# Gate and up products of a feed-forward layer by Strassen's seven products, with three-pass float32 matmuls

## The reference

```
h = _layernorm(x, axis=-1) * (1 + cb) + sb
x = x + gb * _L0_ffn_ref(h, L0_ffn_w_gate, L0_ffn_w_up, L0_ffn_w_down)
...
gate = jnp.einsum('bsd,hd->bsh', x, w_gate)
up = jnp.einsum('bsd,hd->bsh', x, w_up)
gated = jax.nn.silu(gate) * up
return jnp.einsum('bsh,dh->bsd', gated, w_down)
```

## Time and profile before

| | |
|---|---|
| median of 3 runs | 1060.18 us (1058.08 to 1065.53) |
| the profiled execution | 1063.38 us |
| its span | 1061.6 us |
| PE busy | 1022.6 us, 96% |
| DVE, ACT, POOL busy | 626.2, 375.0, 225.8 us |
| granted TensorE clock | 0.995 of full speed |
| projections, recurrence, feed-forward | 0 to about 340, to about 505, from 517 us |

### The profile page before, as it was taken

The page is one execution under the profiler, slowest core; times in us unless marked ns, Lnnn a source line. Parts: engine busy times, 40 slices in busy tenths (PEclk is TensorE's granted clock), DMA queues, the critical chain, the costliest instruction groups (busy, mean ns, idle before and its releaser), DMA issues.

```text
span 1061.6 us, 20179 instructions
## 1 busy us (share of the span) xinstructions
PE 1022.6 (96%) x8112; PEld 822.1 (77%) x8112; DVE 626.2 (59%) x997; ACT 375.0 (35%) x685; POOL 225.8 (21%) x178
## 2 busy tenths in 40 slices
PE   6999999999998999998899999999999999999998
PEld 4676777777676888887777887888888888888886
DVE  5977377899855787878664333343333334334366
ACT  3676674445445343333453112211212212112110
POOL 1322530022025555554301000000000000004191
PEclk9999999999999999999999999999999999999999
DMA  6604336838256666775520001010100101001223
GB/s 212 196 14 135 73 80 165 247 100 215 64 125 170 141 153 146 188 187 130 174 72 28 1 1 60 1 60 1 33 28 1 60 1 58 2 0 70 80 80 119
DMA packets 153438, 97.42 MB, mean 92 GB/s; under 512 B 93569, under 2 KB 130689, under 8 KB 153217
## 3 DMA queue, kind: packets, MB, share of 16 engines
q1 hardware_dynamic: 153344, 96.12, 32.9%
HBM read 64.64 MB, written 31.46 MB: 91 GB/s over the span
## 4 chain that ended last, share of the span: by engine, by line
PE 73%; DVE 10%; DMA 5%; issue 4%; ACT 4%; SPq 4%; POOL 0%; DVEq 0%; ACTq 0%
PE ps L1302 70%; ACT t L1665 3%; PE ps L1310 3%; DVE t L1936 2%; DVE t L2046 2%; DMA scrU<-t 2%; SPq L1179 1%; DVE t L2034 1%; PE ps L1539 1%; DVE t L1941 1%; DVE t L2146 1%; DVE t L1946 1%; DMA scrA<-t 1%; SPq L1239 1%; DMA t<-scrA 1%
## 5 line engine op out<-in xcount | busy, mean ns | idle before, releaser
L1302 PE MATMUL ps<-t,t 128*128 128x512 f32 (+6 forms) x7292 | 969.7, 325 | 30.4 <-DVE t L1936 8.5
L1302 PEld LDWEIGHTS ps<-t,t 128*128 128x128 f32 (+4 forms) x7292 | 769.6, 159 | 215.1 <-issue 43.8
L1936 DVE TENSOR_TENSOR t<-ps,t 128x512 f32<-128x512 f32 (+2 forms) x288 | 199.6, 710 | 245.8 <-PE ps L1302 219.5
L1665 ACT ACTIVATE t<-t 128x512 fp32r<-128x512 f32 (+10 forms) x339 | 189.1, 579 | 308.8 <-DVE t L1936 206.2
L1936 DVE TENSOR_TENSOR t<-t,t 128x512 fp32r<-128x512 f32 (+14 forms) x210 | 168.1, 805 | 114.0 <-ACT t L1665 106.6
L1665 ACT ACTIVATE t<-ps 128x512 f32<-128x512 f32 (+5 forms) x202 | 109.1, 551 | 303.0 <-PE ps L1302 285.1
L2427 POOL TENSOR_TENSOR t<-t,t 128x512 f32<-128x512 f32 x16 | 22.5, 1408 | 375.2 <-DVE t L1936 373.1
L2046 DVE SCALAR_TENSOR_TENSOR t<-ps,t,t 128x511 f32<-128x511 f32 (+2 forms) x108 | 80.2, 747 | 3.3 <-ACT t L1665 0.5
L1665 ACT ACTIVATE t<-ps,t 128x512 f32<-128x512 f32 (+2 forms) x93 | 54.5, 617 | 26.1 <-PE ps L1310 13.0
L1310 PE MATMUL ps<-t,t 128*128 128x128 f32 (+1 forms) x340 | 52.3, 285 | 4.2 <-DVE t L1941 2.1
L1310 PEld LDWEIGHTS ps<-t,t 128*128 128x128 f32 (+1 forms) x340 | 38.1, 146 | 13.5 <-issue 5.5
(11 more groups left out here) (52 smaller groups left out, 257.2 us busy)
## 6 DMA issues: line engine op xcount, KB each, us to landing
scrU<-t SPq DMA_DIRECT2D x60, 256.0 KB, 2.9
t<-in_wf SPq DMA_DIRECT2D x16, 768.0 KB, 4.4
t<-scrU SPq DMA_DIRECT2D x32, 288.0 KB, 5.0
t<-scrU SPq DMA_DIRECT2D x32, 192.0 KB, 3.6
t<-in_W SPq DMA_DIRECT2D x19, 256.0 KB, 3.0
t<-in_x SPq DMA_DIRECT2D x16, 256.0 KB, 4.0
t<-in_wmod SPq DMA_DIRECT2D x4, 1024.0 KB, 6.3
t<-in_x SPq DMA_DIRECT2D x32, 128.0 KB, 2.9
```

The costliest lines, as they stand in the source:

```text
L1302: return e.matmul(o, l, r_, start=start, stop=stop, skip_group_check=True)
L1665: return e.activation(o, i, f, **kw)
L1936: return e.tensor_tensor(o, a, b, op)
```

## The change

Gate and up are computed by Strassen's scheme in Winograd's form. A block of 256 hidden units x 512 inputs is cut into 2 x 2 pieces of 128 x 256, two sequences of 512 tokens (1024 columns) into 2 x 2 pieces of 256 x 512. Seven products of such pieces (6 matmuls each) take the place of eight. The products are added in PSUM: `GU` gives for each the product's number and its bank (0 to 2 for gate, 3 to 5 for up). Products 1, 6, 7 and 4 are added one on another in the first bank, and between them ACT copies the bank's state out (`copy_s`); DVE adds these copies to the other two banks (`cadd`). That gives four output tiles: three come out of `cadd`, the fourth is the first bank itself.

The weights' sums and differences are made on POOL (`w_comb`, 4 instructions of 256 columns for gate and 4 for up), the high parts on ACT (`w_high`, 1792 columns), the low parts on POOL (`w_low_ff`, 7 pieces of 256 columns; `w_high_d` for down, 4 pieces). The activations' sums are made on POOL (`t_raw`) and DVE (`t4`), their seven splits by `split_h` (1024 columns each). The feed-forward layer runs in two passes over the weights (16 iterations `it`: 0 to 7 for sequences 0 and 1, 8 to 15 for 2 and 3). Units of sequences 0 and 1 are turned inside the recurrence (`turn_unit`, called with u - 3 at u = 3, 4, 7, 8, 11, 12 and with 12 and 13 at u = 15) and scaled on ACT; the tiles of sequences 2 and 3 are turned in iterations 1 and 2. The ring of the down product has two banks (6 and 7). The first half of the output is stored at iteration 8.

```diff
@@ -751,6 +739,8 @@
             step("po_sq", u=u - 1)
             step("po_ln", u=u - 1)
             step("po_os", u=u - 1)
+        if u == 15:
+            turn_unit(12)
         if has_tail:
             step("po_yg", u=u - 2)
             step("po_add", u=u - 2)
@@ -787,6 +777,10 @@
                 step("po_xn", u=u - 2)
             if u < 16:
                 step("load_xb", u=u)
+        if u in (3, 4, 7, 8, 11, 12):
+            turn_unit(u - 3)
+        if u == 15:
+            turn_unit(13)
         if has_post:
             ringed("po_wo", u - 1, ("v_yg", u))
         if u < 14:
...
+    GU = [(1, 0), (2, 1), (6, 0), (5, 2), (7, 0), (4, 0), (3, 2)]
+    A_OF = {1: 1, 2: 2, 6: 5, 5: 4, 7: 0, 4: 3, 3: 6}
+    B_OF = {1: 0, 2: 1, 6: 2, 5: 3, 7: 4, 4: 5, 3: 6}
...
+    def down(it, k):
+        i, free = ring_bank()
+        step("down", it=it, k=k, bank=i, free=free)
+        tick("down")
+        ring_free[i] = [tick("v_y")]
+        if it == 7:
+            step("post_0", k=k)
+        if it == 14:
+            step("out_pre", k=k)
...
+    def turn_tile(n):
+        i, free = ring_bank()
+        step("c_turn", n=n, bank=i, free=free)
+        t = tick("norm_tr")[1]
+        step("c_mod", n=n, bank=i, turned=t)
+        ring_free[i] = [tick("a_cmod")]
...
+    def iteration(it):
+        n, last, turn = 2 * it, it == 15, it == 7
+        if it:
+            prod(n, 0)
+            prod(n, 1)
+            copy_s(n, 0)
+            if it != 8:
+                flush()
+            prod(n, 2)
+            cadd(n, 0)
+            prod(n, 3)
+            copy_s(n, 1)
+            flush()
+            step("silu", it=it, t=0)
+            prod(n, 4)
+            if it != 8:
+                down(it - 1, 0)
+            copy_s(n, 2)
+            cadd(n, 1)
+            w_high(up_m(it), [("prod", 7 * (n - 1) + 7)])
+            step("silu", it=it, t=1)
+            w_load_next(it, w_low_ff(up_m(it)))
+            prod(n, 5)
+            prod(n, 6)
+            step("silu", it=it, t=2)
+            cadd(n, 2)
+            step("silu", it=it, t=3)
+            if it == 8:
+                down(7, 0)
+        if not last:
+            w_comb(gate_m(it + 1))
+        for k in range(1, 7):
+            if it and (it < 15 or k < 4):
+                down(it - 1, k)
+            if it in (1, 2) and k in (1, 2, 3, 4):
+                turn_tile(4 * it - 4 + k - 1)
+                if 4 * it + k - 3 < 8:
+                    step("load_xf", n=4 * it + k - 3)
+            if it == 3 and k in (2, 4):
+                gate_row(k // 2 - 1)
+            if it == 12 and k in (2, 4):
+                gate_row(k // 2 + 1)
+            if it and not last and k == 3:
+                next_gate(it, [("prod", 7 * n + 7)])
+        if not last and not turn:
+            w_comb(up_m(it + 1))
...
+        prod(n, 4)
+        if it and not last:
+            down(it - 1, 7)
+        copy_s(n, 2)
+        cadd(n, 1)
...
+        def rest():
+            if turn:
+                for t in range(4):
+                    gated(it, t)
+                    fh(it, t)
+                    if t == 1:
+                        w_high_d(it)
+                    fl(it, t)
...
+                ah = [WGh[up][:, i, kk * 128:kk * 128 + 128] for kk in range(2)]
+                al = [WGl[up][:, i, kk * 128:kk * 128 + 128] for kk in range(2)]
+                if first:
+                    e.wait_ge(*at_least(hi))
+                for kk in range(2):
+                    mm(dst, ah[kk], HSh[j][:, kk, :], kk == 0 and o in (0, 1, 3), False)
+                    mm(dst, al[kk], HSh[j][:, kk, :], False, False)
+                if first:
+                    e.wait_ge(*at_least(lo))
+                for kk in range(2):
+                    t = mm(dst, ah[kk], HSl[j][:, kk, :], False, kk == 1)
+                t.then_inc(sem("prod"), 1)
...
+                for k in range(4):
+                    for b in range(2):
+                        t = act(HR[k // 2][b][:, k % 2, c * 64:c * 64 + 64], src[:, k * 128 + 64 * b:k * 128 + 64 * b + 64],
...
+            elif kind == "w_low_ff":
+                m = st["m"]
+                for tok in st["free"]:
+                    e.wait_ge(*at_least(tok))
+                in_order()
+                for i in range(7):
+                    t = e.tensor_tensor(WGl[m % 3][:, i, :], WR[st["slot"]][:, i, :], WGh[m % 3][:, i, :].bitcast(f32),
```

935 lines of the change are left out of this document (542 added, 393 removed).

## The result

The changed kernel took **1079.12 us** (median of 4 runs, 1077.92 to 1080.28) against 1060.43: 1.017 times as long, 95% interval 1.013 to 1.021. Slower by more than 1%, and outside my range (1040 to 1074, forecast 1059). Its profiled execution took 1080.1 us, with a span of 1078.0 where my sum said 1060.3. I look for 17.7 us.

A forecast was written before the change was run, and what follows sets the result against it. TensorE, busy in 96% of the span, was taken as the bound. Seventh product's end 547.9 + matmuls 469.2 + turned tiles 4.8 + gate rows 5.4 + stalls 28.8 + end 4.2 = 1060.3 us of span; forecast 1059, range 1040 to 1074.

The forecast's parts named there:

- step 4, the stalls: TensorE's waits in the feed-forward stage after the first seventh product, summed over five places: 28.8 us, say 29.
- What hides the rest: Feed-forward stage: GpSimd's pieces take 17 us of a period of about 30.8, weight chains ending 5 to 6 us early.
- Recurrence: Six units with a turn: ScalarE's scalings make VectorE's reduction 4.0 us later, 2.8 us lost each, 16.6 us in all.
- Way to the seventh product: Start of the feed-forward stage: splits and sums on VectorE; seventh product ends at 531.3 on the old clock, 547.9 with turns.
- TensorE's work from there: After the first seventh product: 2070 matmuls, 469.2 us, plus turned tiles 4.8 and gate rows 5.4; period about 30.8 us.
- Seventh product: VectorE evicts the down product ahead of the sum the seventh product needs: 0.35 us, 27 times, 9.5 us.
- Iteration 8: Sixth product waits 7.1 us for ScalarE's copy behind four deferred inputs; splits add 0.7 and 1.2: 9.0 us.
- Iteration 15: Only three downs between gate and up, and GpSimd has an output operation ahead of up's low parts: 1.4 us.
- GpSimd becomes the bound: Slower rival, 0.22: feed-forward weight chains on GpSimd end too late; each 1 us costs 15 us over the kernel, 1074.
- The lists bite less: Faster rival, 0.30: turns cost only TensorE's 0.60 us, so 1046; 1039 if the hole at iteration 8 closes too.
- the 43.5 us: Gate and up: 1344 matmuls instead of 1536, 192 fewer at 0.2267 us; the gain if nothing else changed.

The follow-up runs named there:

- late scaling: The changed kernel with ScalarE's eight scalings of each turned unit moved behind the next slot's decay factors and squares; 1067.9 us.
- sum first: The changed kernel with VectorE's sum for the seventh product put ahead of the down product's eviction; 1073.9 us.
- inputs pipelined: The changed kernel with iteration 7's deferred inputs in the other iterations' pipelined order, GpSimd's down-weight low part ahead of its combinations for up; 1079.8 us.
- hole filled: The changed kernel with 34 needless matmuls of 512 columns ahead of the sixth product in iteration 8; 1079.3 us.
- low parts cut short: The changed kernel with GpSimd's low parts of gate and up weights, iterations 1 to 15, made in 16 of each 256 columns; 1068.1 us.
- fastest version: The changed kernel with scalings late, sums first, raw differences spread and first, last iteration reordered, long GpSimd instructions, 34 needless matmuls in iteration 8; 1050.5 us.
- all but one instruction: The changed kernel with scalings late, sums first, inputs pipelined, combinations behind additions, raw differences spread and first, last iteration reordered; 1053.8 us.
- one instruction: The changed kernel with GpSimd's seven low parts of a weight tile made as one instruction of 1792 columns; 1075.1 us.

## Why the prediction was wrong

The mechanism of each saving and of the turns was right; **what failed is step 4, the stalls, and under "What hides the rest" the sentence that gives GpSimd 17 of 30.8 us as if its work were even.** Point by point:

- *Recurrence* (16.6 us): 13.6 measured (6 x 2.26). Burst 2.48 for 2.6, reduction 3.1 instead of 4.0 us later, 2.3 of it reaching TensorE. Shown by the late scaling, which gave 1.8 back per unit. The condition for "wrong", units under 13 us, did not occur.
- *Way to the seventh product*: 3.3 us too short; which of its many short waits is to blame is open. The clock was at 0.50 here too (512.5 to 515.5 and 529.5 to 532.5, 3.1 us of longer matmuls; 1.00 in the kernel before), but that is not it: in three kernels of the same code there (sum first, inputs pipelined, hole filled) it was 5.6 to 5.9 us, and the last unit to up 1 took 67.1 to 67.4 us, no more than the changed kernel's 67.9.
- *TensorE's work from there*: right; period 30.7.
- *Seventh product* (9.5): 0.27 instead of 0.35 a place, and nothing in iterations 7 to 9; 4.2 by removal.
- *Iteration 4, not in my list*: 4.7, of which 3.4 without the clock. I had read the diff's block of 3 x 1024 columns and never asked where it stands in GpSimd's list; 8.0 us in one piece, with the down weights' low part behind it. An average hides such a block.
- *Iteration 8* (7.1 + 0.7 + 1.2): 15.4 for 9.0. The wait for ScalarE was there, where and why I said, 8.4 for 7.1. To it came half clock, of which filling the hole gave back 0.7, and VectorE and GpSimd late for iteration 9. And it was no wait that could be taken away by reordering: shorter work of GpSimd alone gave 2.4 us, of VectorE and GpSimd together 5.1. That ScalarE is short of time there as well was not tried.
- *Iteration 15* (1.4): the wait was 1.48. Not foreseen: 1.79 for the first evictions behind VectorE's last inputs, 1.0 us for the lower clock behind it, and evictions one every 1.70 us near the end (1066.77, 1068.46, 1070.16) because the addition beside GpSimd took 1.06 instead of 0.69. That makes some 4 of the 5.7 us; the rest I can't place.
- *Clock*: no term at all. TensorE's matmuls took 1.6 + 3.0 + 1.7 = 6.3 us longer behind the three waits, and 1.3 + 0.7 + 1.0 = **3.0 of the 17.7 us** came of it, by kernels in which the clock stayed up. I priced a wait at its own length.
- *Rivals*. "GpSimd becomes the bound" had the sign, not the mechanism, and a price of 1074: it asked for a weight chain too late in every iteration, 15 times 1 us, and the steady iterations never waited for GpSimd (low parts cut short: same period). TensorE waited for it in iterations 4 and 15, and in iteration 9 once the hole was gone: places where work beside the weights is in its list. TensorE waiting for GpSimd in every iteration, my second condition for "wrong", did not occur either. "The lists bite less" fell with the turned units.

The largest parts of what ate the 43.5 us, and 18.7 more, were iterations 7 to 9 (15.4), the turned units (13.6), the last iteration (8.5 over its products and its end), the seventh products (7.3 at 0.27 each, 4.2 by removal) and iteration 4 (4.9). The fastest version keeps 9.8 of the 43.5.

## What to carry to other kernels

Price a wait of TensorE at its length, and at what the clock may cost behind it: here 1.3, 0.7 and 1.0 us more behind waits of 3.1, 8.4 and 1.8 us, and nothing in executions in which the clock did not fall. Before you put a difference of 1 or 2 us down to an edit, compare the granted clock of the same stretch in both kernels. When work is given to an engine that has room on average, lay out its list in the places where one-off blocks stand (set-up, halves' changes, the end), with what is due behind each. And if several reorderings leave a stretch as it was, stop reordering and measure it with less work.

## What the runs showed of the hardware

- **Clock.** Behind 8.4 us of waiting the granted clock was 0.50 for 6 us; with 34 needless matmuls in the wait it was 1.00 throughout, and the stretch 0.7 us shorter. Behind the same wait of 3.1 us of the same code it fell in ten executions of twelve. And what a fall costs depends on who sets the pace: 1.3 us of 1.7 (iteration 5), 1.0 of 1.7 (the end), nothing to be seen of 3 to 6 at the start.
- **One long GpSimd instruction holds up a tiny one of VectorE.** In the fastest version, around the first product: VectorE's operation of 6 columns, else 0.17 us, beside GpSimd's low part in one instruction of 1792 columns. The timeline joins two such operations and what lies between them; the row by form has the first alone, and the last row is TensorE's wait behind it.

```profile
511.80 3.98 POOL L2682 TENSOR_TENSOR t<-t,t 128x1792 fp32r<-128x1792 f32 x1 [0.17 <-POOL t L2702]
511.93 5.00 DVE L2173 TENSOR_TENSOR t<-t,t 128x6 f32<-128x6 f32 x2
```

```profile
L2173 DVE TENSOR_TENSOR t<-t,t 128x6 f32<-128x6 f32 x1 | 3.9, 3864 | 0.0
```

```profile
516.99 1.01 PE L1456 MATMUL ps<-t,t 128*128 128x512 f32 x2 [4.23 <-DVE t L2173]
```

With pieces of 256 columns at the same place, in the kernel "all but one instruction":

```profile
511.40 4.86 POOL L2689 TENSOR_TENSOR t<-t,t 128x256 fp32r<-128x256 f32 x4 [0.17 <-POOL t L2709]
511.54 1.75 DVE L2179 TENSOR_TENSOR t<-t,t 128x6 f32<-128x6 f32 x2
```

```profile
L2179 DVE TENSOR_TENSOR t<-t,t 128x6 f32<-128x6 f32 x1 | 0.6, 620 | 0.0
```

```profile
513.35 0.73 PE L1465 MATMUL ps<-t,t 128*128 128x512 f32 x2 [0.99 <-DVE t L2179]
```

3.86 us against 0.62, and a wait of 4.23 against 0.99: 3.2 of the 3.5 us lost at the start. The Trainium skill (SBUF — State Buffer, on the shared port pair) says that either engine holds the pair for its whole instruction; the trace agrees, in its length too. It is a matter of what meets what. In the kernel "one instruction" the long low part of the start (523.29 to 527.35) met no operation of 6 columns, and the last unit to up 1 took 66.5 us, not more than with pieces; in the fastest version the raw differences go first and the low part starts just ahead of one. In the feed-forward stage the long instruction cost nothing that shows: VectorE's reads of PSUM on the path took 687 ns either way. Long instructions there and pieces at the start were not run together.
- **GpSimd's cost per piece.** 1792 columns in one took 4.06 us, 256 took 0.77 and 16 columns 0.22.
